# Both norms ahead of the expert layers with tokens on partitions: one product centres, turns and routes

## What is computed

```python
mod = (_silu(L0_c) @ L0_wmod).reshape(L0_c.shape[0], 6, 1, -1)
sa, ca, ga, sb, cb, gb = ...
h = _layernorm(x) * (1 + ca) + sa
x = x + ga * _L0_attn_ref(h, ...)          # selective scan
h = _layernorm(x) * (1 + cb) + sb          # the norm of this case
x = x + gb * _L0_ffn_ref(h, Wr, br, W1, b1, W2, b2)
```

## Time and profile before

| | |
|---|---|
| median of 3 runs | 1242.08 us (1236.18 to 1242.45) |
| the profiled execution, span | 1241.9 us |
| PE busy | 1122.4 us, 90% |
| DVE busy | 873.1 us, 70% |
| ACT busy | 808.9 us, 65% |
| POOL busy | 304.4 us, 25% |
| mean granted clock of PE | 0.939 |

### The profile page before, as it was taken

One profiled execution on the slowest core, in us unless ns is written; L12 is line 12 of the kernel. 1 busy time (PEld: TensorE's weight loads), 2 busy tenths in 40 slices (PEclk: granted clock), 3 DMA queues, 4 the chain that ended last, 5 costly groups with the idle time before them and its releaser, 6 DMA issues.

```text
span 1241.9 us, 21389 instructions
## 1 busy us (share of the span) xinstructions
PE 1122.4 (90%) x7770; PEld 545.3 (44%) x7770; DVE 873.1 (70%) x1663; ACT 808.9 (65%) x1215; POOL 304.4 (25%) x312
## 2 busy tenths in 40 slices
PE   9747779798987899999999999999999999989885
PEld 6412227598853233333333333333333332477884
DVE  2599985568046888889898888888888881363223
ACT  3653323276444688888898898888888899431222
POOL 0079850477534200000000000000000000006773
PEclk7969997799879799999999999999999999978997
DMA  2055510488433301100111011100111000007983
GB/s 103 1 186 195 201 52 34 164 274 271 131 142 109 108 28 37 37 18 20 37 36 36 2 36 37 37 15 23 36 37 32 2 4 4 3 35 248 298 258 125
DMA packets 50348, 107.17 MB, mean 86 GB/s; under 512 B 9796, under 2 KB 12132, under 8 KB 49860
## 3 DMA queue, kind: packets, MB, share of 16 engines
q1 hardware_dynamic: 44166, 93.89, 23.2%
q0 software_dynamic: 4992, 10.23, 2.8%
q10 hardware_dynamic: 1086, 1.68, 0.4%
HBM read 92.41 MB, written 12.94 MB: 85 GB/s over the span
## 4 chain that ended last, share of the span: by engine, by line
PE 62%; issue 11%; DVE 7%; DMA 7%; ACT 7%; POOL 4%; SPq 1%; POOLq 0%; DVEq 0%; ACTq 0%
PE psum L946 17%; PE psum L937 16%; PE psum L925 10%; ACT probs L1300 5%; DMA x_got<-xtok_dram,get_row 4%; PE psum L1051 4%; PE psum L1063 4%; PE psum L770 2%; DVE ssm_h L1703 1%; POOL y_dram L1536 1%; PE psum L748 1%; PE psum L1041 1%; DMA y_in<-y_dram 1%; PE psum L761 1%; POOL x_got L1529 1%
## 5 line engine op out<-in xcount | busy, mean ns | idle before, releaser
L1300 ACT ACTIVATE probs<-psum 128x1024 f32<-128x1024 f32 x512 | 496.2, 1023 | 51.7 <-PE psum L937 51.4
L2002 DVE TENSOR_REDUCE tile_max<-psum 128x1 f32<-128x512 f32 x720 | 466.7, 686 | 68.1 <-PE psum L925 62.6
L925 PE MATMUL psum<-k_stack,q_stack 64*128 64x512 bf16 x994 | 333.0, 386 | 10.4 <-DMA q_stack<-q_dram 7.8
L937 PE MATMUL psum<-q_stack,k_stack 64*128 64x512 bf16 x1024 | 284.8, 381 | 4.5 <-DMA q_stack<-shift_rows 0.8
L946 PE MATMUL psum<-probs,v_head 128*32 128x512 f32 x2048 | 272.7, 605 | 0.6 <-ACT probs L1300 0.6
L925 PEld LDWEIGHTS psum<-k_stack,q_stack 64*128 64x128 bf16 x994 | 89.7, 94 | 266.3 <-DVE tile_max L2002 120.7
L1502 POOL TENSOR_TENSOR max_parts<-row_max,no_shift 128x8 bf16<-128x8 f32 x32 | 6.4, 200 | 591.5 <-DVE row_max L1978 591.5
L937 PE MATMUL psum<-q_stack,k_ext 64*128 64x512 bf16 x512 | 144.3, 379 | 0.0
L937 PE MATMUL psum<-q_stack,ln_xc 64*128 64x512 bf16 x512 | 137.6, 376 | 0.0
L1529 POOL DMA_INDIRECT x_got<-xtok_dram,get_row x78 | 76.7, 984 | 103.2 <-issue 60.2
L937 PEld LDWEIGHTS psum<-q_stack,k_stack 64*128 64x128 bf16 x1024 | 70.2, 93 | 53.5 <-ACT probs L1300 31.8
(11 more groups left out here) (273 smaller groups left out, 1350.4 us busy)
## 6 DMA issues: line engine op xcount, KB each, us to landing
w1r<-w SPq DMA_DIRECT2D x78, 256.0 KB, 3.8
w2r<-w SPq DMA_DIRECT2D x78, 256.0 KB, 3.8
ssm_b<-bc_dram SPq DMA_DIRECT2D x32, 512.0 KB, 3.9
k_stack<-k_dram SPq DMA_DIRECT2D x60, 120.0 KB
y_in<-y_dram SPq DMA_DIRECT2D x16, 256.0 KB, 5.3
q_stack<-q_dram SPq DMA_DIRECT2D x30, 96.0 KB
bc_p<-bc_dram SPq DMA_DIRECT2D x5, 512.0 KB, 5.3
k_stack<-k_dram SPq DMA_DIRECT2D x30, 80.0 KB
```

Source lines behind the costliest of these rows:

```text
L925: mm(bank, queries, k_stack[rows, u, keys:keys + C], start=True, stop=True).then_inc(s1_ps, 1)
L937: return mm(psum[:, 2 * slot + side, :], k[side_rows(side), kt * 128:(kt + 1) * 128], q_stack[side_rows(side), u, part, at:at + C], start= ...
L1300: f(probs[:, kt % 4, hf * HALF:(hf + 1) * HALF], banks(2 * slot, 2), ACT.Exp, scale=SCALE).then_inc(p_ready, 1)
L2002: v.tensor_reduce(top, bank, AX.X, ALU.max).then_inc(s1_read, 1)
```

## The change

The two norms ahead of the expert layers are done with tokens on partitions. A matrix `token_w` is made once: identity minus 1/128 (which centres) in its 128 middle columns, and beside them, for each layer, the router's weights scaled by 1 + cb and centred. For each tile PE makes one product of `xT`'s tile with 136 of its columns (`turn_tokens`): 128 centred features and 8 raw logits, token by token. DVE takes the variance of each token with `bn_stats` and works out 1/std for all 2048 tokens at once (`token_stats`). ACT copies the centred features to `x_tok` with 1/std as scale (`token_rows`). Scale and shift of the norm move to where a block's columns are copied to `x_cols`. DVE multiplies the raw logits by 1/std, adds a bias `logit_b`, and chooses the top two from the shifted logits, for all tiles at once; exp is taken afterwards, of all logits in layer 0 and of the second logit alone in layer 1, and the gates are worked out behind the row numbers. `ssm_out` writes banks 4 to 7. The idle products inside the norms go; 12 stand ahead of the count. Making `token_w` and `logit_b` is put into `ssm_inputs`. Cut to its core:

```diff
@@ ssm_inputs, PE @@
                 pe.wait_ge(mats_loaded, 16)
+                pe.wait_ge(v_ready, NC)
+                pe.wait_ge(token_w_step, 2)
+                mm(psum[:, 7, 0:2 * NE], token_w[:, NE:NE + 128], scaled_w[:].rearrange("p n e -> p (n e)"), start=True, stop=True)
+                for n in range(2):
+                    i = mm(psum[:, 7, (2 + n) * NE:(3 + n) * NE], modc(n, SB).to_broadcast([128, 128]), router_w[n], start=True, stop=True)
+                i.then_inc(mod_ps_ready, 1)
                 for c in range(NC):
...
+                    if c == NC - 1:
+                        pe.wait_ge(token_w_step, 6)
                     mm(psum[:, c, :], mat("W_dt"), chunk(uT, c), start=True, stop=True).then_inc(dt_bc_ps, 1)
@@ PE @@
-            def route(layer, c):
...
+            def turn_tokens(layer):
                 done = (1 + 2 * layer) * NC
+                for t in range(TILES):
+                    if t % TPC == 0:
+                        pe.wait_ge(ln_in_ready, done + t // TPC + 1)
+                    if t % 2 == 0 and t >= TILES // 2:
+                        pe.wait_ge(ln_in_ready, done + (t - TILES // 2) // 2 + 1)
+                    mm(whole_bank(layer, t), xT[:, t * 128:(t + 1) * 128], token_ws[layer], start=True, stop=True,
+                       skip_group_check=True).then_inc(tok_ps, 1)
...
             def place(layer):
-                for t in range(TILES):
-                    i = mm(psum[:, t // TPC, t % TPC * 128:(t % TPC + 1) * 128], normT[:, t * 128:(t + 1) * 128], mat("ident"),
-                           start=True, stop=True)
...
+                pe.wait_ge(tok_copied, TILES * layer + 8)
+                busy(psum[:, 3, :], 12)
                 pe.wait_ge(place_ready, placed(layer)["either"])
@@ ACT @@
-            def route(layer):
...
+            def token_rows(layer):
+                table(ACT.Sqrt)
+                act.wait_ge(tok_step, 3 * layer + 1)
+                f(tok_var["std"][:], tok_var["var"][:], ACT.Sqrt, bias=eps_col[:]).then_inc(tok_std_ready, 1)
+                act.wait_ge(tok_step, 3 * layer + 3)
+                for t in range(TILES):
+                    f(x_tok[:, t, :], token_bank(layer, t), ACT.Identity, scale=tok_var["rstd"][:, t:t + 1]).then_inc(tok_copied, 1)
+                act.wait_ge(shifted_ready, layer + 1)
+                if layer == 0:
+                    f(rt["prob"][:], rt["logit"][:], ACT.Exp).then_inc(exp_ready, 1)
+                else:
+                    f(second_gate[:], rs["top2"][:], ACT.Exp).then_inc(exp_ready, 1)
                 table((ACT.Silu, ACT.Gelu)[layer])
...
-                    f(x_cols[:, i % COL_RING, :], psum[:, 4 + i % 2, 0:128], ACT.Identity).then_inc(cols_ready, 1)
+                    f(x_cols[:, i % COL_RING, :], psum[:, 4 + i % 2, 0:128], ACT.Identity, scale=modc(0, CB), bias=modc(0, SB)).then_inc(cols_ready, 1)
@@ DVE @@
+            def token_stats(layer):
+                for c in range(NC):
+                    dve.wait_ge(proj_ps, NC * layer + c + 1)
+                    dve.wait_ge(x_biased, layer + 1)
+                    v.scalar_tensor_tensor(chunk(xT, c), psum[:, 4 + c, :], modc(layer, GA), chunk(xT, c),
                                            ALU.mult, ALU.add).then_inc(ln_in_ready, 1)
+                for t in range(TILES):
+                    dve.wait_ge(tok_ps, TILES * layer + (t | 1) + 1)
+                    i = v.bn_stats(tok_stats[:, t, :], token_bank(layer, t))
+                step(i)
+                step(v.tensor_tensor(tok_var["sum"][:], tok_stats[:, :, 2], tok_stats[:, :, 5], ALU.add))
+                step(v.tensor_tensor(tok_var["half"][:], tok_stats[:, :, 1], tok_stats[:, :, 1], ALU.mult))
+                v.scalar_tensor_tensor(tok_var["var"][:], tok_var["sum"][:], 1.0 / D, tok_var["half"][:], ALU.mult, ALU.add).then_inc(tok_step, 1)
+                dve.wait_ge(tok_std_ready, layer + 1)
+                v.reciprocal(tok_var["rstd"][:], tok_var["std"][:]).then_inc(tok_step, 1)
...
             def ssm_inputs():
+                dve.wait_ge(router_loaded, 48)
+                v.tensor_tensor(token_w[:, NE:NE + 128], mat("ident"), mat("mean"), ALU.subtract).then_inc(token_w_step, 1)
...
+                dve.wait_ge(mod_ps_ready, 2)
+                v.tensor_copy(token_w[:, 0:NE], psum[:, 7, NE:2 * NE]).then_inc(token_w_step, 1)
+                v.tensor_copy(token_w[:, 128 + NE:128 + 2 * NE], psum[:, 7, 0:NE]).then_inc(token_w_step, 1)
+                v.tensor_tensor(logit_b[:, 0, :], psum[:, 7, 2 * NE:3 * NE], router_b, ALU.add).then_inc(token_w_step, 1)
+                v.tensor_copy(logit_b[:, 1, :], psum[:, 7, 3 * NE:4 * NE]).then_inc(token_w_step, 1)
...
+            def route(layer):
...
+                i = v.tensor_tensor(logit[:].rearrange("p (b s) e -> p b s e", s=2), raw_logits(layer),
+                                    tok_var["rstd"][:].rearrange("p (b s) -> p b s", s=2).unsqueeze(3).to_broadcast([128, 8, 2, NE]), ALU.mult)
+                i.then_inc(tok_step, 1)
+                dve.wait_ge(tok_step, 3 * layer + 3)
+                dve.wait_ge(token_w_step, 6)
+                step(v.tensor_tensor(logit[:], logit[:], each(logit_b[:, layer, :]), ALU.add))
+                step(v.tensor_reduce(rs["max"][:], logit[:], AX.X, ALU.max))
+                step(v.tensor_tensor(logit[:], logit[:], wide(rs["max"]), ALU.subtract))
+                step(v.scalar_tensor_tensor(rt["eq"][:], logit[:], 0.0, each(expert_no), ALU.is_ge, ALU.mult))
+                lowest(0)
+                step(v.scalar_tensor_tensor(rt["rest"][:], masks[:, 0], LOWEST, logit[:], ALU.mult, ALU.add))
+                i = v.tensor_reduce(rs["top2"][:], rt["rest"][:], AX.X, ALU.max)
+                i.then_inc(shifted_ready, 1)
+                dve.wait_ge(shifted_ready, layer + 1)
+                step(v.tensor_tensor(rt["eq"][:], rt["rest"][:], wide(rs["top2"]), ALU.is_equal))
+                step(v.tensor_tensor(rt["eq"][:], rt["eq"][:], each(expert_no), ALU.mult))
+                lowest(1)
...
-                    v.tensor_copy(x_cols[:, n % COL_RING, :], psum[:, 4 + n % 2, 0:128]).then_inc(cols_ready, 1)
+                    v.tensor_scalar(x_cols[:, n % COL_RING, :], psum[:, 4 + n % 2, 0:128], modc(1, CB), modc(1, SB), ALU.mult, ALU.add).then_inc(cols_ready, 1)
```

More of the change, by code:

```diff
@@ L754, in var @@
                     c = n % NC
-                    if returned is None and first and not (routed is not None and c >= 2):
-                        busy(psum[:, 4 + c, 128:C], 2)
                     pe.wait_ge(ln_sq_ready, n + 1)
@@ L1163, in std @@
                     f(ln_std[:, c % 2, :], psum[:, 4 + c, 0:TPC], ACT.Sqrt, bias=eps_col[:]).then_inc(ln_std_ready, 1)
-                    if following is not None and c == NC - 1:
-                        table(following)
                 def scaled(n):
@@ L1331, in attention @@
                 store_chunks(act, NH - 1, LAST_BY_ACT)
-            def place(layer):
-                for c in range(NC):
-                    act.wait_ge(tok_ps, NC * layer + c + 1)
-                    f(x_tok[:, c * TPC:(c + 1) * TPC, :].rearrange("p t d -> p (t d)"), psum[:, c, :], ACT.Identity).then_inc(tok_copied, 1)
             def hidden(n):
```

189 lines of the change are left out of this document (79 added, 110 removed).

## The result

| | before | after |
|---|---|---|
| median, first comparison | 1240.48 us (4 runs, 1236.18 to 1242.45) | 1209.56 us (4 runs, 1205.93 to 1217.56) |
| ratio, 95% interval | | 0.9752 (0.971 to 0.9795) |
| profiled execution, span | 1241.9 us | 1204.1 us |
| mean granted clock of PE | 0.939 | 0.960 |
| PE busy | 1122.4 us | 1076.3 us |

The change takes 30.9 us off the median; the forecast was 27.4 off, 1214.5 us. So the first thing to ask is which part of 37.8 us belongs to the change.

The account below looks back on a forecast made before the run. Two serial chains of residual, norm and routing, stretches of 29.6 and 29.2 us, set when all behind them starts. Savings of 14.1 + 13.5 - 0.2 = 27.4 us from 1241.9 gave 1214.5 us, range 1206.5 to 1224.

Parts of the forecast that it names:

- each stretch: Residual, norm and routing of one layer, POOL's first cast to the count: 27.2 and 26.6 us, to save 14.1 and 13.5.
- Rival 3: Block loops start on something that does not follow the count, so the gain is given back: 1238 to 1242 us, chance 0.05.
- rival 4: PE comes cold to the block loops and stays at half clock, 1.5 us a block: 1259 to 1331 us, chance 0.03.
- Residuals: All four residual additions stand ahead of the statistics; the last ends 0.75 us after POOL's first cast.
- PE's turning products: 16 fp32 products of `xT` tiles with a 136-column matrix, some 4.1 us at full clock, beside the statistics.
- The statistics: Sixteen `bn_stats` over 128 columns of PSUM on DVE, 0.25 us each, 4.0 us a layer; bounds 0.20 and 0.70.
- rival 2: `bn_stats` is dear, say 0.5 us each, 4 us more in each layer: 1222.5 us, at 0.70 us 1228.9; chance 0.17.
- Small steps: After the statistics, three tiny DVE steps, ACT's square root and a reciprocal: 1.05 us.
- the idle products at half clock: Ahead of the count, behind PE's gap of 4.5 us, ten slow and two fast products: 4.75 us, count at 200.15.
- Rival 1: The clock holds through PE's gap, the count comes 2.0 us sooner in each layer: 1210.4 us, chance 0.20.
- The loops' pointers: Scale and shift in block column copies: 0.18 us on ACT, 0 to 0.05 on DVE, POOL sets the pace; 0.2 us taken.
- The block biases: Three more steps, 0.9 us, stand ahead of them in layer 0, hidden by 4.3 us of cover before first read.

Follow-up runs that it names:

- early_idle: The changed kernel with the 12 idle products ahead of the count started after two copies of `x_tok` instead of eight, in both layers: 1206.80 us, 0.9753 of before.
- stats_twice: The changed kernel with each of the 16 row statistics a layer taken a second time into a tensor nobody reads: 1217.49 us, 0.9835 of before.

## Why the prediction was right

**The frame.** That each stretch is a serial chain, and that all behind it moves with its end, held: the medians fell by 28.8 to 30.9 us and the two stretches by 28.4 to 29.3. Rival 3 (gain given back) and rival 4 (loops that stay at half clock) did not come; the loops were no longer than before. That the two sums fit this closely is in part luck, since layer 1's stretch of before alone has been seen at 26.6 and at 24.3 us.

**The terms, from POOL's first cast, forecast and measured in layer 0.** Residuals end at +0.75, measured +0.65: the four stand together, 3.04 us. PE's turning products 4.1 us, measured 3.87. The statistics 4.0 us, measured 3.53, and rival 2, the dear statistic, is out with 0.20 us each where nothing holds them up. The estimate of 0.26 us a piece from the Trainium skill (VectorE: DVE Perf Modes, section on the TRN2 errata) is near the 0.28 us that one of them lasts here, but they start 0.20 to 0.22 apart, so its sum of 4.1 us was farther off than mine. Small steps 1.05 us, measured 1.28 (189.94 to 191.22): the root on ACT is 0.31 and not 0.25 (DVE waits 0.37 us for it), and the reciprocal 0.25 and not 0.17. The first scaled copy at +6.12, measured +5.74. `either` at +10.66, measured +10.33. So the chain was 0.3 to 0.4 us shorter than the sum, most of it from the statistics.

**The clock.** The step with most risk was the idle products at half clock, 4.75 us, with a count 2 us behind `either`. Measured in layer 0: 4.45, 5.30 and 5.30 us, and in the two latter traces the count is at +13.06, exactly the forecast distance. That it is exact is luck: the products started 0.34 us sooner than forecast, took 0.55 us longer, and the count starts some 0.2 us ahead of their recorded end. Layer 1 had 4.36 to 4.45 us and the count at 12.23 to 12.32, against 13.07. Rival 1 (full clock) did not come in any trace of after, though early_idle showed it once. What the forecast did not draw from this was the edit: if 12 idle products come cold and late, they should go.

**What was costed at nothing.** The loops' pointers: 0 to 0.05 us on DVE was wrong, it is 0.12 (0.410 against 0.291), but POOL's pace covers it, as said. The block biases: I gave them 4.3 us of cover. They end 217.86 + 1.45 = 219.31 and the first silu is at 221.15, so 1.8 us were left. The three added steps took some 0.8 us of it (distance from the count 21.2 against 20.4 us), and the first silu comes 1.7 us sooner behind the count (23.05 against 24.77): 0.6 because the second gather, for which PE waits, landed sooner (21.6 against 22.2 us behind the count), and 1.1 because PE's products ahead of the silu ran at full clock in this trace, where before had half (first two rows, before; then after).

```profile
236.42 0.79 PE L1041 MATMUL psum<-mats,x_got 128*128 128x128 f32 x2 [3.77 <-DMA x_got<-xtok_dram,get_row]
237.01 1.92 PE L1051 MATMUL psum<-x_cols,w1r 128*128 128x128 f32 x8
...
217.86 1.45 DVE L1866 TENSOR_REDUCE block_b<-b_of 128x156 f32<-128x1248 f32 x1
219.67 0.49 PE L1060 MATMUL psum<-mats,x_got 128*128 128x128 f32 x2 [3.38 <-DMA x_got<-xtok_dram,get_row]
220.00 1.06 PE L1070 MATMUL psum<-x_cols,w1r 128*128 128x128 f32 x8
...
221.15 1.14 ACT L1388 ACTIVATE hid<-psum,block_b 128x128 f32<-128x128 f32 x4 [0.49 <-PE psum L1070]
```

The first stage: behind the start of the last convolution step, ACT's reader comes after 5.73 us in before and 5.74 in after, and POOL's first cast after 133.3 us in all fourteen traces. So the four added copies and the pass that waits for them cost nothing, as forecast. The first cast came at 187.1 to 187.4 in the three traces with the old norm and at 183.0 to 187.7 in the eleven with the new one; all of that arises ahead of the convolution, where it goes with the clock, as shown above. A small cost of the work added there could hide in it.

**The size.** 27.4 us forecast, 29 to 31 measured. The forecast time, 1214.5, was counted from the span of 1241.9, which is 1.4 above the median that the result is held against; its low end, 1206.5, is 0.3 lower than its own terms give (1208.8 - 2 = 1206.8). The two stretches were forecast to save 27.6 and saved 28.4 to 29.3: the statistics, 0.3 to 0.4 us a layer, and idle products of 4.4 us in place of 4.75 in layer 1 (and in layer 0 of one trace). The rest, 0.4 to 1.6 us, is less than the medians of before themselves differ by, 1236.6 to 1240.5.

## What to carry to other kernels

When a kernel ends a stage with a string of short steps on several engines, count the passes across engines first: one product that centres, turns and routes at once, and statistics with tokens on partitions, took off some 24 us by subtraction, where a leaner choice of experts took 4. Products that only keep TensorE's clock up must be measured by what they hold back: behind a pause they may run at half clock themselves and gate the work that they were to help. And compare medians before comparing traces: of 37.8 us between two executions, 6.9 were not there in the medians, and the stages that gave them differ in their granted clock.

## What the runs showed of the hardware

- `bn_stats` over 128 columns of PSUM lasts 0.28 us and started every 0.20 us where nothing held it up (stats_twice); a copy of 128 columns of PSUM on DVE is 0.29.
- A pointer operand for scale and one for bias add 0.18 us to a 128-column ACT copy (0.277 to 0.458) and 0.12 us to one on DVE (0.291 to 0.410).
- A bf16 result of 128 elements written across on DVE took 0.70 us and in order 0.29. Read across by PE, the same 128 columns took 0.39 us where they took 0.27, both at a granted clock of 0.50.
- The granted clock was still 1.00 in 4.4 us without work and 0.54 in the work behind; after pauses of 2.85 us it was 0.60 once and full once.
- The same 140 products of the old norm in layer 1 took 26.61 us at a mean granted clock of 0.74 and 24.26 at 0.86, and the first block loop took 107.5 us at 0.92 and 102.0 at 0.99.
- One chip runs the first block loop of before in 135 us where the other has 107; the ratio to before is alike on both for the two kernels that ran on both (0.9796 and 0.9790, 0.9756 and 0.9720, with intervals that overlap).
